# Five looping engine programs written out, and waits joined to the work behind them

## The reference, cut to what matters

```python
h = relu(layernorm(x))                               # layer 0
idx = first 25 neighbours of each node, by node number
agg = max over the neighbours of h[idx]              # a node with at most 25: also max with 0
x = x + relu(concat(h, agg) @ W0 + b0)
h = relu(layernorm(x)) @ W1                          # layer 1
e = leaky_relu(s1[:, None] + s2[None, :], 0.4)       # s1 = h @ a1, s2 = h @ a2
att = softmax(where(adj > 0, e, -1e20), axis=1)
x = x + gelu(att @ h)
```

## Time and profile before

| what | us |
|---|---|
| median of 3 runs | 4714.1 |
| lowest and highest of them | 4710.35, 4717.25 |
| the profiled execution: span from first to last instruction | 5921.6 |
| POOL, DVE, PE, ACT busy in it | 3420.3, 3609.4, 2583.7, 2320.3 |

### The profile page before, as it was taken

The page is one execution under the profiler, slowest core; times in us unless marked ns, Lnnn a source line. Parts: engine busy times, 40 slices in busy tenths (PEclk is TensorE's granted clock), DMA queues, the critical chain, the costliest instruction groups (busy, mean ns, idle before and its releaser), DMA issues.

```text
span 5921.6 us, 48215 instructions
## 1 busy us (share of the span) xinstructions
PE 2583.7 (44%) x13568; PEld 1939.9 (33%) x13568; DVE 3609.4 (61%) x6299; ACT 2320.3 (39%) x2505; POOL 3420.3 (58%) x3205
## 2 busy tenths in 40 slices
PE   1332334444445334434455344444445435444357
PEld 1221223333333233323333233333334323333236
DVE  4454557566666566555677555666567656666567
ACT  2121234333444335333354333544335333434248
POOL 3655565555666566664677546466567665665530
PEclk9555556566666676666667666666666667666679
DMA  4434434344444444444444444344444444443322
GB/s 148 131 114 135 133 120 132 111 132 144 144 128 125 132 152 127 129 125 140 149 143 153 134 130 142 111 135 152 143 124 152 134 136 148 138 129 122 118 75 71
DMA packets 397876, 775.86 MB, mean 131 GB/s; under 512 B 64739, under 2 KB 245862, under 8 KB 381286
## 3 DMA queue, kind: packets, MB, share of 16 engines
q0 software_dynamic: 153600, 419.64, 23.8%
q1 hardware_dynamic: 244070, 353.77, 18.1%
HBM read 689.26 MB, written 83.89 MB: 131 GB/s over the span
## 4 chain that ended last, share of the span: by engine, by line
another core or an unknown queue 34%; issue 17%; ACT 14%; PE 12%; DVE 9%; POOL 1%; DMA 0%; ACTq 0%; DVEq 0%; SPq 0%; POOLq 0%
PE ps_av L895 4%; PE ps_l L923 3%; ACT stage L390 2%; ACT lk L444 2%; ACT lk L451 2%; ACT nbt L437 2%; PE ps_l L941 1%; ACT sg L384 1%; DVE hl L657 1%; DVE val L717 1%; PE ps_l L924 1%; POOL gb L372 1%; PE ps_l L943 1%; ACT y L498 1%
## 5 line engine op out<-in xcount | busy, mean ns | idle before, releaser
L372 POOL DMA_INDIRECT gb<-h_table,idx x3200 | 3419.6, 1069 | 2275.2 <-DVE gb L657 1039.9
L895 PE MATMUL ps_av<-hz,lk 128*128 128x256 f32 x3840 | 1136.2, 456 | 158.1 <-issue 85.7
L895 PEld LDWEIGHTS ps_av<-hz,lk 128*128 128x128 f32 x3840 | 878.6, 235 | 403.5 <-issue 252.5
L934 PE MATMUL ps_t<-cf,y 128*128 128x128 f32 x256 | 84.3, 430 | 2055.4 <-ACT y L498 1615.6
L388 ACT ACTIVATE sg<-ps_c 128x2048 bf16<-128x2048 bf16 x128 | 240.2, 1877 | 1813.7 <-remote 1673.1
L735 DVE SCALAR_TENSOR_TENSOR lk<-val,lk 128x2048 f32<-128x2048 f32 (+1 forms) x240 | 421.2, 1755 | 674.9 <-ACT lk L444 613.2
L657 DVE TENSOR_REDUCE hl<-gb 128x256 f32<-128x3328 f32 x128 | 746.8, 5834 | 83.6 <-DMA gb<-h_table,idx 67.2
L657 DVE TENSOR_REDUCE gb<-gb 128x256 f32<-128x3328 f32 x128 | 741.0, 5789 | 30.9 <-DMA gb<-h_table,idx 26.0
L934 PEld LDWEIGHTS ps_t<-cf,y 128*128 128x128 f32 x256 | 36.0, 197 | 2080.2 <-ACT y L498 1634.1
L923 PE MATMUL ps_l<-w,hcat 128*128 128x256 f32 x1024 | 407.2, 567 | 600.6 <-ACT hcat L485 505.2
L923 PEld LDWEIGHTS ps_l<-w,hcat 128*128 128x128 f32 x1024 | 277.5, 284 | 693.1 <-ACT hcat L485 483.4
(11 more groups left out here) (95 smaller groups left out, 3767.9 us busy)
## 6 DMA issues: line engine op xcount, KB each, us to landing
ad<-in_adj SPq DMA_DIRECT2D x128, 1024.0 KB
edge<-edges_t SPq DMA_DIRECT2D x128, 512.0 KB
gb<-h_table,idx POOLq DMA_INDIRECT x3200
edges_t<-stage SPq DMA_DIRECT2D x32, 1024.0 KB
xl<-in_x SPq DMA_DIRECT2D x128, 128.0 KB
hl<-h_table SPq DMA_DIRECT2D x128, 128.0 KB
x_rows<-x SPq DMA_DIRECT2D x128, 128.0 KB
xo<-x_rows SPq DMA_DIRECT2D x16, 1024.0 KB
```

Of the source, the lines that this page charges most:

```text
L372: pool.indirect_dma_start(gb[c][:, s + (c > 0), :], None, table[tb], bass.IndirectOffsetOnAxis(idx[u][:, k:k + 1], 0)).then_inc(gathered[c ...
L895: ins = T.matmul(ps_av[:, k * C:(k + 1) * C], lk_of(jj, u, drain)[:, k * P:(k + 1) * P], hz[jj][:, :], start=False, stop=False)
```

## The change

Every loop is written out: each engine's program becomes one straight list of all rounds and steps. Round and step numbers are then plain numbers, so every value that a wait compares with and every offset of a DMA or an operand is a constant. `wait_apart` is deleted; each of its places becomes a plain `wait_ge`, without the increment, that can be carried by the instruction behind it. `SECTIONS` and the three `_passed` semaphores go. The order of the work on every engine, all operands, buffers and semaphores that are read stay as they are.

```diff
-        SECTIONS = {False: [(0, 0, 1), (2, 1, 3), (6, 3, 4), (8, 4, 5), (10, 5, 7), (14, 7, 8)],
-                    True: [(0, 0, 1), (2, 1, 4), (8, 4, 5), (10, 5, 6), (12, 6, 7), (14, 7, 8)]}
-        def wait_apart(engine, name, semaphore, value):
-            engine.wait_ge(semaphore, value)
-            engine.sem_inc(S[name], 1)
...
             def store_hn(tb, k, m, u, src):
-                wait_apart(sp, "sp_passed", S["hn_ready"], m + 1)
+                sp.wait_ge(S["hn_ready"], m + 1)
...
-            with sp.Fori(2, NB - 2, 2) as b:
-                round_(b, 0)
-                round_(b + 1, 1)
-            round_(NB - 2, 0)
+            for b in range(2, NB - 1):
+                round_(b, b % 2)
...
-            with pool.Fori(0, NB, 2) as b2:
-                for tb in range(2):
-                    b = b2 + tb
-                    for u in range(2):
-                        wait_apart(pool, "pool_passed", hn_stored[u], b * 64 + 64)
-                    with pool.Fori(0, PAIRS) as i:
-                        for u in range(2):
-                            g = b * TILES + i * 2 + u
-                            wait_apart(pool, "pool_passed", S["idx_ready"], g + 1)
-                            k = 0
-                            for c, n in enumerate(CHUNKS):
-                                wait_apart(pool, "pool_passed", maxed[c], g + 1)
-                                for s in range(n):
-                                    pool.indirect_dma_start(...)
+            for b in range(NB):
+                tb = b % 2
+                for u in range(2):
+                    pool.wait_ge(hn_stored[u], b * 64 + 64)
+                for t in range(TILES):
+                    g, u, k = b * TILES + t, t % 2, 0
+                    pool.wait_ge(S["idx_ready"], g + 1)
+                    for c, n in enumerate(CHUNKS):
+                        pool.wait_ge(maxed[c], g + 1)
+                        for s in range(n):
+                            pool.indirect_dma_start(...)
...
                 if find_words:
-                    wait_apart(dve, "dve_passed", S["words_read"], a + 1)
+                    dve.wait_ge(S["words_read"], a + 1)
...
-                if not (type(i) is int and i < 2):
-                    wait_apart(dve, "dve_passed", S["leaky_ready"], i - 1)
-                wait_apart(dve, "dve_passed", S["blocked_ready"], i + 1)
+                if not (i < 2):
+                    dve.wait_ge(S["leaky_ready"], i - 1)
+                dve.wait_ge(S["blocked_ready"], i + 1)
...
-                for t0, i0, end in SECTIONS[last]:       # on ACT, DVE and PE alike
-                    if end == i0 + 1:
-                        pair(i0, t0)
-                    else:
-                        with dve.Fori(i0, end) as i:
-                            pair(i, t0)
+                for i in range(PAIRS):
+                    pair(i, 2 * i)
...
-            with dve.Fori(2, NB - 1) as b:
+            for b in range(2, NB - 1):
                 round_(b)
```

More of the change, by code:

```diff
@@ L243, in _ @@
             sp.sem_inc(S["edges_stored"], 16)
-            wait_apart(sp, "sp_passed", S["ones_ready"], 1)
+            sp.wait_ge(S["ones_ready"], 1)
             for tb in range(2):
@@ L282, in step @@
                     if t == 15:
-                        wait_apart(sp, "sp_passed", S["edges_stored"], 16 * 4 * eb + 16 * 5)
+                        sp.wait_ge(S["edges_stored"], 16 * 4 * eb + 16 * 5)
                     if w:
-                        wait_apart(sp, "sp_passed", S["blocked_ready"], (b - 1) * 32 + 2 * t)
+                        sp.wait_ge(S["blocked_ready"], (b - 1) * 32 + 2 * t)
                     load_edge(eb, nt, nt % 2)
-                if l and not (type(b) is int and b == NB - 1 and t == 15):
-                    wait_apart(sp, "sp_passed", S["cat_transposed"], v)
-                    wait_apart(sp, "sp_passed", S["stats_ready"], PAIRS + v)
+                if l and not (b == NB - 1 and t == 15):
+                    sp.wait_ge(S["cat_transposed"], v)
+                    sp.wait_ge(S["stats_ready"], PAIRS + v)
                     if t == 15:
                         for k in range(2):
-                            wait_apart(sp, "sp_passed", hn_stored[k], b * 64 + 128)
+                            sp.wait_ge(hn_stored[k], b * 64 + 128)
                         load_l(1 - tb, b + 1, 0, 0)
@@ L306, in step @@
                     if t == N_FIRST:
-                        wait_apart(sp, "sp_passed", maxed[1], b * TILES + 1)
-                        wait_apart(sp, "sp_passed", S["cat_transposed"], b * TILES)
+                        sp.wait_ge(maxed[1], b * TILES + 1)
+                        sp.wait_ge(S["cat_transposed"], b * TILES)
                     store_hn(1 - tb, t - N_FIRST, m, u, xn[u][:, :, :])
@@ L330, in round_ @@
                          l=not drain, e=(not first or t == 15) and not (drain and t == 15),
-                         w=not first and not (type(b) is int and b == 1 and t == 0), last=last)
+                         w=not first and not (b == 1 and t == 0), last=last)
                     if not first:
-                        if t == 1 and not (type(b) is int and b == 1):
+                        if t == 1 and not (b == 1):
                             store_out(b - 2, 1, b * 2 - 3)
@@ L351, in _ @@
             store_out(NB - 1, 1, 2 * NB - 1)
-            wait_apart(sp, "sp_passed", S["out_stored"], 16 * 2 * NB)
+            sp.wait_ge(S["out_stored"], 16 * 2 * NB)
         @block.gpsimd
@@ L518, in step @@
                     act.wait_ge(S["h_done"], v + 1)
-                    if not (type(b) is int and b == 0):
+                    if not (b == 0):
                         act.wait_ge(S["s_copied"], b)
@@ L532, in pair @@
                         t = t0 + u
-                        one = type(b) is int and b == 1
+                        one = b == 1
                         fl = {1: b * 2 - 3, 9: b * 2 - 2}.get(t) if not first and not (one and t == 1) else None
@@ L756, in take_s1 @@
                 dve.wait_ge(S["h_saved"], b * TILES)
-                if not (type(b) is int and b == 1):
+                if not (b == 1):
                     dve.wait_ge(S["val_ready"], (b - 1) * 32)
@@ L783, in step @@
                     if t == 1:
-                        wait_apart(dve, "dve_passed", S["h_copied"], b)
+                        dve.wait_ge(S["h_copied"], b)
                     item_rows(o, it - 2, j2, 0, before)
@@ L825, in step @@
                     if not t:
-                        wait_apart(dve, "dve_passed", S["s_copied"], b)
+                        dve.wait_ge(S["s_copied"], b)
                     item_bounds(o, it, j)
@@ L899, in open_sweep @@
             def open_sweep(f):
-                if not (type(f) is int and f == 0):
+                if not (f == 0):
                     pe.wait_ge(S["gelu_done"], f)
@@ L965, in pair @@
                         step(b, i, u, t, a=not drain and not (last and t >= 12), l=not drain,
[L966 to L972, removed]
+                             old=not first and not (b == 1 and t == 0), drain=drain)
+                for i in range(PAIRS):
+                    pair(i, 2 * i)
             round_(0, first=True)
             round_(1)
-            with pe.Fori(2, NB - 1) as b:
+            for b in range(2, NB - 1):
                 round_(b)
```

33 lines of the change are left out of this document (15 added, 18 removed).

## The result

The changed kernel is slower: 4726.4 us against 4711.4 us for the kernel before, medians of 19 runs each; the ratio is 1.0029 with a 95% interval of 1.0022 to 1.0035. I had forecast 4708 us and no change or a small gain.

A forecast was written before the change was run, and what follows sets the result against it. POOL, gathering almost without a break, was taken as the bound; from 4714.1 us, -6 us for the rounds' back edges and 0 for all other terms gave 4708 us, likeliest case 4690 to 4720, 8 in 10 4635 to 4740.

The forecast's parts named there:

- What bounds the kernel: POOL, unprofiled, gathers almost without a break at some 34.6 us a step; the other engines follow, DVE 7.1 us under it.
- Rival A: The cycle DVE - PE - ACT sets the step and POOL's sum is a coincidence: 4629 us, chance 0.20.
- PE's late semaphores: At L388 ACT waited 1673.1 us in 98 waits, read as PE's semaphores coming late while its records are taken.
- the gathers' 0: On POOL, 3200 gathers before and after with the same operands, already in straight code inside the loop body: 0.
- Register instructions and separate waits: 0: On DVE, ACT, PE and SP, at most 129 us, all beside POOL's gathers on engines 7 to 17 us under it: 0.
- POOL's waits and loops: 0: 400 semaphore instructions and 64 loop ends on POOL, 20 us if all on the path, hidden by gathers in flight: 0.
- Instruction code: 0: POOL's longer program, about 15 packets, fetched behind the gathers: 0, or +74 us if each packet stalled POOL.
- rival C: POOL's long code stalls it at each new packet: up to 74 us slower, 4788 us if whole, 4750 if half; chance 0.12.
- Back edges: -6: Rounds' branches at L976 on PE, DVE and ACT: 20 us if POOL waited for the whole; -6 us taken, bounds 0 and -20.
- The end: 0: Last 225.5 us, POOL done, ACT busy, then PE takes over; sequencer work hides behind a busy engine: 0, bounds 0 and -10.
- Rival B: POOL does wait at rounds' starts and behind separate waits; most of the missing 39.7 us go: 4679 us, chance 0.13.
- my sum for the kernel before: POOL's gathers and gaps 4395.3 us, start 53.6, end 225.5: 4674.4 us, 39.7 us (0.8%) under the runs' median.

## Why the prediction was wrong

**What bounds the kernel** was right. The profile after shows POOL without a break, as I had read it out of a stretched profile: between its gathers lie the ordinary gaps and next to nothing else. Rival A is out. That PE's late semaphores belonged to the profiled execution and not to the kernel is borne out as far as every later profile lacks them; what made that one execution late is open. None of the kernels with a single engine's loops shows it.

**The step that failed** is the sentence that the change touches neither the gathers nor the operations beside which they stall, and with it the gathers' 0. Measured, the gathers cost 13.8 us more (3482.6 against 3468.8 with DVE's loops back), 28 us lost at one place and some of it won back elsewhere; what I had set as the sign of being right, gathers of about 1069 ns and a sum of about 4670 us, came out at 1088 ns and 4720.9 us. The instructions are the same, but not when they start, and the price of a stall depends on that to a tenth of a microsecond. The trace before held it: in the earlier trace rows the gather of 3029.61 started 0.26 us after L735 and took 2.84 us, that of 3040.80 started 0.53 us after its own L735, which stands in the same timeline, and took 2.58 us:

```profile
3040.27 2.28 DVE L735 SCALAR_TENSOR_TENSOR lk<-val,lk 128x2048 f32<-128x2048 f32 x1
```

0.27 us later, 0.26 us less. I saw two stalls, not a slope. I named the phase between gathers and DVE only as an uncertainty of the range.

**Register instructions and separate waits: 0.** The cover was there, and still the step was wrong: I counted what their removal could give back on DVE, and not what an earlier DVE does to POOL. That an instruction is hidden says that its time costs nothing, not that its place is free. The separate waits by themselves were 0, as priced (DVE alone 1.0028, all 1.0027, both like the change).

**POOL's waits and loops: 0** was right (1.0031 and 1.0040 with them back, as without), but not by the cover that I named, gathers in flight. In the trace with POOL's loops back 66 of 68 loop branches run while no gather does, in the gap between two; that gap is 0.303 to 0.312 us there, the ordinary one, so they fit into it. **Instruction code: 0** was right: no gap between two gathers of the changed kernel is above 0.3 us but at the waits shown, so rival C, the slower one, had the right side by the wrong mechanism. The Trainium skill's rule that I had set against it (Runtime: NRT & Kernel Launch, "Instruction fetch mechanics") held for POOL.

**Back edges: -6** wasn't found; that the change saves POOL about as much elsewhere is luck. With PE's loops back alone PE's round branches take up to 6.6 us (first row), yet POOL's gaps come to 977.5 us against 976.4 in the changed kernel, and at no round's start is one longer than the ordinary one. With DVE's loops back POOL waits 17.7 us in 36 waits for the maxima, against 8.6 us in 23 in the changed kernel (second row):

```profile
L963 PEldq COMPARE_BRANCH  x5: 76/5872/6588, 1711.0 to 3972.4; - x5
...
POOL gb L367 <- DVE gb L648: 17.7, 36, 1.9
```

Each of these waits contains an ordinary gap, so what the change saves there is the difference of all gaps, 981.2 against 976.4: 5 us, beside the 13.8 us that the gathers lose. The nine gaps above 0.36 us stand before tiles 12 and 14 of a round, none at its edge. What the edges of all engines together cost isn't shown, since the one trace that has them is the stretched one. **The end: 0** was right as well, 208.3 us after the last gather, 208.2 with DVE's loops back; but the earlier trace rows don't show PE taking over from ACT, which is the busier one in both stretches (48.86 against 43.10 of 50 us in the later).

Rival B's 35 us are in none of the unstretched profiles: what the gaps between gathers hold above the ordinary is under 6 us in each. What my sum for the kernel before lacked was, as far as the kernel with DVE's loops back stands for it, more stalls: its gathers take 3468.8 us against 3419.6 in the stretched profile, while its end is 17 us shorter (208.2 against 225.5). That a POOL that never waits meets DVE more often is how I read this.

What wasn't tried: joined waits with the loops kept.

## What to carry to other kernels

Where one engine stalls another for as long as an instruction runs, count the collisions, but also look where in the other's cycle each begins: the price can be a sawtooth, and then making the free engine a little faster costs, a little slower costs more, and slower still pays. When a change only removes hidden instructions, ask which instructions start earlier by it and what they now run into. And sum the bound engine's stalled instructions before and after: in all 13 unstretched profiles here the span is this sum and 1236 to 1243 us more. But a sum is that of one execution. Among the eight kernels that have DVE's loops written out and no pause it runs from 3480.9 to 3494.9 us, so a difference of 15 us has to be borne out by the medians, or by a place in the step where nothing scatters.

## What the runs showed of the hardware

The gather needs DVE out of the way only at its start: one that has begun when the two-input operation begins keeps its 0.95 us (in the changed kernel's first rows above, one started at 2383.58 and ran 0.95 us, past the addition's start at 2384.34), and the addition isn't longer for it (median 2.276 us in the 91 that began during a gather, 2.277 in the 21 others). One that begins inside the operation ends 0.82 us after the operation's end, wherever in it it began (0.814 to 0.830 us over the changed kernel's 224 full-width operations of rounds 1 to 7 at which a gather stalled).

Length alone doesn't stall: 1124 gathers of the changed kernel begin inside one of DVE's maxima (L639, one input, 5.8 us each) and take 0.947 us on average, like undisturbed ones. The operations with two inputs over 1024 or 2048 columns make up 442 of the 455 us that its gathers lose. One operation with a single input does stall: six gathers that begin inside the copy of 2048 columns (L741, 1.22 us) take 1.72 us on average. The Trainium skill (SBUF — State Buffer, section "SBUF: two separate sides") has the lock: of a VectorE operation with two SBUF inputs and a GpSimd one that reads SBUF, the first takes the port pair for the whole instruction and the other is blocked. The trace agrees for the gather that comes second, and differs for the operation that comes second, which isn't held.
